# Starting the K-stack transfers from ScalarE, at steps 1 and 7 of a unit, in place of the SP queue

## The chip, the cores and the metric

The kernel runs on one core of a Trainium2 chip. The metric is the device time in microseconds (us) of one execution; lower is better.

## What is computed

One gated cross-attention layer and one gated feed-forward layer, over 8 batches of 224 tokens of width 1024, with a context of 8 x 750 tokens. Cut to what matters:

```python
q = x @ Wq.T;  k_raw = context @ Wk.T;  v_raw = context @ Wv.T      # 32 heads of 32
q = _rmsnorm(q);  k = _rmsnorm(k)                                   # per head
attn = softmax(einsum('bhnd,bhmd->bhnm', q, k) * HEAD_DIM ** -0.5)
out = einsum('bhnm,bhmd->bhnd', attn, v)
x = x + tanh(g_xattn[0]) * xattn(layernorm(x), ctx, Wq, Wk, Wv)
hidden = sigmoid(h @ Q(w1).T) * (h @ Q(w2).T)                        # h = layernorm(x), Q: ternary weights
x = x + tanh(g_ffn[0]) * (hidden @ Q(w3).T)
```

## The kernel before

There are three phases. Phase A projects the queries and stores them in DRAM. Phase B, which holds the change, projects keys and values and attends. The last phase is the feed-forward layer.

Phase B runs over 32 units, `u` = 0 to 31: four groups `g` of eight heads, each over eight batches `b`. A unit has 24 steps `r`, written as `t, j = r // 4, r % 4`: six context tiles `t` of 125 tokens, and four steps `j` for each. In every step TensorE does a quarter of the projection of tile `t` of unit `u` (L1255), then the scores of an earlier unit's piece (L1273), then the products of attention weights and values of a still earlier piece (L1297, L1300). The scores of unit `u - 1` begin at step 8 of unit `u` (`SHIFT`), and the value products trail them by three steps (`LAG`). Two more rounds, `k == U` and `k == U + 1`, finish the attention; in them nothing is projected.

All engines run their own program in order and are coupled by semaphores alone. In a step, piece `e` of the scores goes through this chain: scores on TensorE (step e + 8), `exp` on ScalarE (L831, same step), `phi`, its 16-bit high half, on ScalarE (L822, one step later), `plo`, the rest, on VectorE (L1102, same step as `phi`), and the value products on TensorE (step e + 11). At steps with `j == 1` ScalarE also rounds the next context tile (`chi`, L755) ahead of `phi`, and VectorE subtracts (`clo`, L987) ahead of `plo`. At steps with `j == 3` ScalarE copies `val` (L797) and `knat` (L801) ahead of `phi`; at steps 7 and 15 VectorE also sums a weight block (`gsum`, L1096) ahead of `plo`.

The normalised keys of a tile are transposed and copied by VectorE into `kpair` (L1083, at `j == 2` two tiles later). From there four DMAs in each of two parts gather them into `kst`, the K stacks that the scores read: part 0 holds tiles 0 to 3 of a unit (four DMAs of 250 KB), part 1 tiles 4 and 5 (four DMAs of 125 KB). Tile 3 of unit `u - 1` is in `kpair` after step 22 of unit `u - 1`; tile 5 after step 6 of unit `u`. TensorE waits for part 0 at step 8 and for part 1 at step 10 of unit `u` (L1266).

All DMAs go through the SP queue (`@block.sync`), in program order. For a unit `u` it issues: context loads `craw` for each `t` (L337, each waits until VectorE is done with the slot), at `t == 1` the save of an attention result (L354) and in the last five units a layer-norm save and load (L385, L386, L375, L379, called `ln_save` and `ln_load`), at `t == 2` a weight block `gbuf` (L430), at `t == 3` part 0 and at `t == 4` part 1 of the K stacks of unit `u - 1` (L396), then again `ln_save` and `ln_load`, and at `t == 5` eight loads of `qT` (L416), which wait until the scores of unit `u - 2` are over at step 7. The layer-norm tiles of batches that are finished are worked in units 27 to 31 (`ln` is true), in the gaps of the attention work.

Of the kernel before, what the change touches and what calls it, by code (L numbers as in the profile page):

```python
# [21 lines left out]
KT, KW = 6, 125  # L22
G, HG = 4, 8
GC = HG * DH
U = G * B
NQ = 4 * KT
# [5 lines left out]
HD2 = 2 * DH  # L32
# [24 lines left out]
def flamingo_kernel(nc, x_d, ctx_d, wq_d, wkv_d, wffn_d, gates_d, out_d):  # L57
# [8 lines left out]
    def sem(name):  # L66
        return top.enter_context(nc.semaphore(name))

    def sb(scope, name, shape, dt):
        return scope.enter_context(nc.sbuf_tensor(name, shape, dt))  # L70

    with top:
# [57 lines left out]
        kst = sb(pb, "kst", [P, 2, HG, SK], F16)  # L130
# [15 lines left out]
        kpair = sb(pb, "kpair", [P, 2, NP, SK], F16)  # L146
# [58 lines left out]
        kst_in = [[sem(f"kst_in{i}_{h}") for h in range(2)] for i in range(2)]  # L205
# [7 lines left out]
        s_ready = sem("s_ready"); p_ready = sem("p_ready"); phi_ready = sem("phi_ready")  # L213
# [39 lines left out]
        def projects(k):  # L253
            return k < U
# [53 lines left out]
        def _(sp):  # L308
# [25 lines left out]
            def load_ctx(T, slot, idx):  # L334

                wait(sp, clo_ready, T - 2)
                sp.dma_start(craw[:, slot, :, :], ctx_d[idx, :, :, :]).then_inc(ctx_in[slot], 16)  # L337
# [11 lines left out]
            def save_att(a, par, qts=(0, 1)):  # L349
                sp.wait_ge(att_ready, 2 * a + 1 + qts[-1])  # L350
                for qt in qts:
                    r0, r1 = QSAVED[qt]
                    q0 = QCOLS[qt].start
                    sp.dma_start(att_d[a, q0 + r0:q0 + r1, :],  # L354
                                 oatt[r0:r1, par, qt, :, :].rearrange("p h d -> p (h d)")
                                 ).then_inc(att_saved[par], 16)

            def load_w(j, s):

                for m in range(3):  # L360
                    sp.dma_start(wraw[:, 1 - s, m, :], wffn_d[m * (FJ // 2) + j, :, s, :]).then_inc(w_in[s], 16)

            def ln_load(i):

                s, b = ln_slot(i), i // 2
                if ln_slot(i) == 0:
                    sp.wait_ge(wklo_ready, KC * G)
                else:
                    sp.wait_ge(kv_ready, KT * U)


                sp.wait_ge(att_saved[b % 2], 32 * (((G - 1) * B + b) // 2 + 1) - (16 if i == NL - 2 else 0))
                wait(sp, ln_saved[s], 32 * ln_uses(i))
                cx, ca, _ = ln_mem[s]
                sp.dma_start(cx[:, :], x_d.rearrange("i p d -> (i p) d")[i * LT:i * LT + LT, :]  # L375
                             ).then_inc(lx_in[s], 16)
                for g in range(G):
                    r0 = LT * (i % 2)
                    sp.dma_start(ca[:, GC * g:GC * g + GC], att_d[g * B + b, r0:r0 + LT, :]).then_inc(lx_in[s], 16)  # L379

            def ln_save(i):
                s = ln_slot(i)
                _, ca, cn = ln_mem[s]
                sp.wait_ge(cnl_ready, i + 1)
                sp.dma_start(x1_d[i * LT:i * LT + LT, :], ca[:, :]).then_inc(ln_saved[s], 16)  # L385
                sp.dma_start(cn_d[i * LT:i * LT + LT, :, :], cn[:, :, :]).then_inc(ln_saved[s], 16)  # L386

            def stack_k(v, part):

                t0, t1 = ((0, 4), (4, KT))[part]  # L390
                sp.wait_ge(kpair_ready, v * KT + t1)
                if v >= 2:
                    sp.wait_ge(s_ready, (v - 1) * NQ)
                for i in range(2):
                    for s in range(2):
                        sp.dma_start(kst[HD2 * i:HD2 * i + HD2, v % 2, s:HG:2, KW * t0:KW * t1],  # L396
                                     kpair[HD2 * s:HD2 * s + HD2, v % 2, :, KW * t0:KW * t1]
                                     ).then_inc(kst_in[v % 2][part], 16)

            def unit_b(u, par, k, b, g, ln):  # L400
                if projects(k):
                    for t in range(KT):
                        if k or t >= 3:
                            load_ctx(u * KT + t, (par * KT + t) % 3, b * KT + t)
                        if t == 3 and k >= 1:
                            stack_k(u - 1, 0)
                        if t == 4 and k >= 1:
                            stack_k(u - 1, 1)
                        if t == KT - 1:
                            if k >= 2:  # L410

                                sp.wait_ge(s_ready, (u - 1) * NQ)
                            for i in range(4):
                                for s in range(2):
                                    r0 = HD2 * s + DH * (i // 2)
                                    sp.dma_start(qT[DH * i:DH * i + DH, par, s:HG:2, :],  # L416
                                                 qst_d[g, :, r0:r0 + DH, b * S:b * S + S].rearrange("p r t -> r p t")
                                                 ).then_inc(q_in[par], 16)
                        if t == 1 and k >= 2 and not (isinstance(u, int) and u == 2):
                            save_att(u - 3, 1 - par)  # L420
                        if ln and t in (1, 4):

                            i = 2 * (b - LNLAG) + t // 4
                            if i:
                                ln_save(i - 1)
                            ln_load(i)
                        if t == 2:
                            if k >= 2:
                                sp.wait_ge(gsum_ready, u * 2 - 2)
                            sp.dma_start(gbuf[:, par, :, :], wffn_d[u, :, :, :]).then_inc(gw_in[par], 16)  # L430
                if k == U:
                    load_ctx(U * KT, 0, 0)
                    stack_k(U - 1, 0)
                    sp.wait_ge(gsum_ready, 2 * U - 2)
                    sp.dma_start(gbuf[:, 0, :, :], wffn_d[U, :, :, :]).then_inc(gw_in[0], 16)
                if k == U:
                    save_att(U - 3, 1)
                    stack_k(U - 1, 1)
                    for i in (10, 11):
                        ln_load(i)  # L440
                    ln_save(9)
                    save_att(U - 2, 0)
                    for i in (12, 13):
                        ln_load(i)
                    sp.wait_ge(gsum_ready, 2 * WPAIRS)
                    for i in range(2):
                        for h in range(2):
                            sp.wait_ge(kst_in[i][h], 64 * (U // 2))
                    sp.wait_ge(v3_ready, KT * U + 1)
                    load_w(0, 0)  # L450
                    ln_save(10)
                    ln_save(11)
# [6 lines left out]
            for u in range(U):  # L459
                g = u // B  # L460
                unit_b(u, u % 2, min(u, 2), u % B, g, u >= (G - 1) * B + LNLAG)
                if u == 0 or (u % B == 1 and 0 < g < G - 1):
                    prefetch_w(g + 1)
            unit_b(U, 0, U, None, None, False)
            unit_b(U + 1, 1, U + 1, None, None, False)


# [87 lines left out]
        def _(pool):  # L555
# [96 lines left out]
            def ln_low(i):  # L652
                cx, _, cn = ln_mem[ln_slot(i)]
                pool.wait_ge(cnh_ready, i + 1)
                pool.tensor_tensor(cn[:, 1, :], cx[:, :], cn[:, 0, :], ALU.subtract).then_inc(cnl_ready, 1)  # L655
# [25 lines left out]
        def _(act):  # L681
# [15 lines left out]
            def w_high(g, kcs=range(KC)):  # L697

                act.wait_ge(wk_in, g * 16 + 16)
                if g:  # L700
                    act.wait_ge(kv_ready, g * (B * KT))
                for kc in kcs:
                    act.activation(wkhi[:, kc, :], wkraw[:, kc, :], ACT.Copy).then_inc(wkhi_ready, 1)
# [43 lines left out]
            def ln_high(i):  # L747
                cx, _, cn = ln_mem[ln_slot(i)]
                act.wait_ge(cn_ready, i + 1)
                act.activation(cn[:, 0, :], cx[:, :], ACT.Copy).then_inc(cnh_ready, 1)  # L750
# [8 lines left out]
            def group_b(g):  # L759
                if not (isinstance(g, int) and g == 0):  # L760
                    w_high(g)

            def unit_b(u, par, k, b, g, ln):
                for r in range(NQ):
                    t, j = r // 4, r % 4

                    Tb = u * KT + (t - 1)
                    pt = (par * KT + t - 1) % 2
# [66 lines left out]
                    if j == (1 if ln else 3):  # L835
                        for i in ln_tiles(u, k, t, ln, "norm"):
                            ln_high(i)

            units(act, unit_b, group_b)


# [578 lines left out]
```

## Time and profile before

| | us |
|---|---|
| median of three runs (2708.07 to 2711.51) | 2710.05 |
| the profiled execution, its own time | 2711.99 |
| its span in the trace | 2710.2 |
| TensorE busy | 2588.1 |
| VectorE busy | 1658.9 |
| ScalarE busy | 1454.9 |
| mean granted TensorE clock, share of full | 0.977 |

The span begins at the first and ends at the last instruction of the trace; the execution's own time is 1.79 us longer. Phase B lasts from about 230 to about 1845 us. Busy time does not hold instructions that issue DMAs.

### The profile page before, as it was taken

The numbers are of one execution on the slowest core, as the hardware profiler recorded it, in microseconds if no ns is written. First come the engines' busy times: TensorE is split into PE (matmuls) and PEld (weight loads), VectorE is DVE, ScalarE is ACT, GpSimd is POOL, SyncE is SP. The second block draws the span as 40 slices with busy tenths as digits, with TensorE's granted clock in tenths as the row PEclk, the third lists the DMA queues.
The fourth block names the chain that finished last, engine by engine and source line by source line (L and its number), as shares of the span: only waits on it lengthen the run. The fifth ranks groups of instructions, "written<-read, shape, count | busy, mean of one in ns | idle before, by whom it ended". The sixth has DMA issues, their size and how long they took to land.

```text
span 2710.2 us, 49526 instructions
## 1 busy us (share of the span) xinstructions
PE 2588.1 (95%) x18370; PEld 1872.0 (69%) x18370; DVE 1658.9 (61%) x2808; ACT 1454.9 (54%) x3102; POOL 928.8 (34%) x865
## 2 busy tenths in 40 slices
PE   7998999999999999999999988875899999999999
PEld 6776888888888888888888877663455455554444
DVE  5665777777777787777777877775544444430000
ACT  3333888888788888878788766673211111110000
POOL 3552344545445444454544755665000000000000
PEclk9998999999999999999999999986999999999999
DMA  4226455555544546446454566757423333334441
GB/s 154 79 63 199 113 152 130 135 127 150 152 125 137 134 114 182 125 131 136 120 151 125 147 163 182 183 140 235 161 96 100 109 107 107 93 98 137 148 123 71
DMA packets 274321, 361.45 MB, mean 133 GB/s; under 512 B 113569, under 2 KB 222625, under 8 KB 269345
## 3 DMA queue, kind: packets, MB, share of 16 engines
q1 hardware_dynamic: 274080, 358.29, 47.0%
q8 instruction: 146, 2.39, 0.4%
q14 instruction: 95, 0.77, 0.1%
HBM read 252.17 MB, written 56.89 MB: 114 GB/s over the span
## 4 chain that ended last, share of the span: by engine, by line
issue 35%; POOL 31%; PE 30%; DMA 2%; DVE 1%; SPq 0%; POOLq 0%; ACT 0%; DVEq 0%
PE ps L1350 19%; POOL krs L607 13%; PE ps L1377 10%; POOL oinv L628 4%; POOL osum L623 3%; POOL kms L603 3%; POOL qrs L585 2%; POOL osum L626 2%; POOL oatt L633 1%; DMA stage<-x_normalised 1%; POOL oinv L630 1%; POOL qms L582 1%; DMA attention<-oatt 1%; POOL cn L655 0%; DMA wraw<-in_wffn 0%
## 5 line engine op out<-in xcount | busy, mean ns | idle before, releaser
L1255 PE MATMUL ps<-wkhi,chi 128*125 128x512 f32 x1536 | 671.3, 437 | 8.9 <-DVE wklo L910 5.0
L1255 PE MATMUL ps<-wkhi,clo 128*125 128x512 f32 x1536 | 610.3, 397 | 0.0
L1255 PE MATMUL ps<-wklo,chi 128*125 128x512 f32 x1536 | 609.6, 397 | 0.0
L1102 DVE TENSOR_TENSOR plo<-pf,phi 125x448 f16<-125x448 f32 x768 | 545.6, 711 | 88.4 <-ACT phi L822 86.9
L831 ACT ACTIVATE pf<-ps 125x448 f32<-125x448 f32 x768 | 418.9, 545 | 291.2 <-PE ps L1273 288.1
L1350 PE MATMUL ps<-xnTh,w12q 128*128 128x512 f16 (+1 forms) x1408 | 481.6, 356 | 3.8 <-ACT xnTh L847 3.8
L1350 PE MATMUL ps<-xnTl,w12q 128*128 128x512 f16 (+1 forms) x1408 | 480.8, 355 | 0.0
L822 ACT ACTIVATE phi<-pf 125x448 f16<-125x448 f32 x768 | 443.9, 578 | 5.3
L1297 PE MATMUL ps<-val,phi 125*128 125x97 bf16 x3072 | 337.1, 210 | 37.7 <-DVE plo L1102 37.5
L607 POOL TENSOR_TENSOR krs<-kms,mhalf 125x8 f32<-125x8 f32 x192 | 345.7, 1801 | 15.1 <-POOL kms L603 0.2
L1255 PEld LDWEIGHTS ps<-wkhi,clo 128*125 128x125 f32 x1536 | 287.1, 187 | 73.7
L987 DVE TENSOR_TENSOR clo<-craw,chi 128x1000 fp32r<-128x1000 f32 x193 | 231.6, 1200 | 170.5 <-ACT chi L755 170.5
L1300 PE MATMUL ps<-val,plo 125*128 125x65 bf16 x3072 | 323.9, 195 | 0.0
L603 POOL TENSOR_TENSOR kms<-kss,rmseps 125x8 f32<-125x8 f32 x192 | 72.3, 377 | 732.0 <-DVE kss L1057 732.0
L1255 PEld LDWEIGHTS ps<-wkhi,chi 128*125 128x125 f32 x1536 | 288.1, 188 | 48.4 <-issue 9.8
L1255 PEld LDWEIGHTS ps<-wklo,chi 128*125 128x125 f32 x1536 | 289.7, 189 | 38.3
L1297 PEld LDWEIGHTS ps<-val,phi 125*128 125x128 f16 x3072 | 265.8, 98 | 44.9 <-DVE plo L1102 38.8
L1273 PE MATMUL ps<-qT,kst 128*125 128x224 f16 x1536 | 277.8, 263 | 17.6 <-DMA kst<-kpair 17.6
L1273 PEld LDWEIGHTS ps<-qT,kst 128*125 128x125 f16 x1536 | 207.1, 137 | 125.3 <-DMA kst<-kpair 20.0
L1377 PE MATMUL ps<-w3q,hid 128*128 128x512 bf16 x1232 | 266.1, 379 | 1.0 <-DVE hf L1136 1.0
L1300 PEld LDWEIGHTS ps<-val,plo 125*128 125x128 f16 x3072 | 252.0, 99 | 0.5
L861 ACT ACTIVATE sg<-ps 128x512 f32<-128x512 f32 x88 | 47.9, 544 | 357.3 <-PE ps L1350 357.3
(95 smaller groups left out, 3302.6 us busy)
## 6 DMA issues: line engine op xcount, KB each, us to landing
craw<-in_ctx SPq DMA_DIRECT2D x193, 500.0 KB, 4.5
gbuf<-in_wffn SPq DMA_DIRECT2D x33, 1024.0 KB, 6.9
wraw<-in_wffn SPq DMA_DIRECT2D x66, 512.0 KB, 5.8
kst<-kpair SPq DMA_DIRECT2D x128, 250.0 KB, 7.3
hid<-hidden SPq DMA_DIRECT2D x7, 2816.0 KB, 12.5
hidden<-hh SPq DMA_DIRECT2D x66, 256.0 KB, 2.1
kst<-kpair SPq DMA_DIRECT2D x128, 125.0 KB, 2.5
qT<-q_pairs SPq DMA_DIRECT2D x256, 56.0 KB, 3.2
```

The lines of the kernel that those rows point to most:

```text
L603: pool.tensor_tensor(kms[0:KW, :], kss[0:KW, :], rmseps[0:KW, 0:HG], ALU.add).then_inc(kms_ready, 1)
L607: pool.tensor_tensor(krs[0:KW, :], kms[0:KW, :], mhalf[0:KW, 0:HG], ALU.pow).then_inc(krs_ready, 1)
L822: act.activation(phi[0:KW, e % 6, :, :], pf[0:KW, e % 6, :].rearrange("p (t n) -> p t n", t=2), ACT.Copy).then_inc(phi_ready, 1)
L831: act.activation(pf[0:KW, e % 6, :], bank(3 + e % 3)[0:KW, 0:2 * S], ACT.Exp, bias=LN128, scale=SCALE).then_inc(p_ready, 1)
L987: dve.tensor_tensor(clo[:, par, :, :], craw[:, slot, :, :], chi[:, par, :, :].bitcast(F32), ALU.subtract).then_inc(clo_ready, 1)
L1102: dve.tensor_tensor(plo[0:KW, e % 6, :, :], pf[0:KW, e % 6, :].rearrange("p (t n) -> p t n", t=2), phi[0:KW, e % 6, :, :], ALU.subtract).t ...
L1255: mm = pe.matmul(bank(pt)[0:KW, :], a[:, pt, kc, :], w[:, kc, :], start=(kc == 0 and n == 0), stop=(kc == KC - 1 and n == 2))
L1273: mm = pe.matmul(bank(3 + e % 3)[0:KW, S * n:S * n + S], kst[:, ap, hd, KW * kt:KW * kt + KW], qT[:, ap, hd, :], start=True, stop=True)
L1297: mm = pe.matmul(o[:, c0:c0 + VW], phi[0:KW, sl, n, q], val[0:KW, vp, kt, hd, :], start=(e % 6 == 0 and qt == 0 and n == 0), stop=False, s ...
L1300: mm = pe.matmul(o[:, c0 + DH:c0 + VW], plo[0:KW, sl, n, q], val[0:KW, vp, kt, hd, DH:VW], start=False, stop=(e % 6 == 5 and n == 1), skip ...
L1350: mm = pe.matmul(o, w12q[:, s, m, kc, :], xt[:, kc, c0:c0 + n], start=(kc == 0 and part == 0), stop=(kc == KC - 1 and part == 1))
L1377: mm = pe.matmul(bank(4 * par + 2 * tt + c), hid[par][:, j, part, P * tt:P * tt + P], w3q[:, j, 512 * c:512 * c + 512], start=(j == 0 and ...
```

## The change

`stack_k` moves from the SP program to the ScalarE program. The two waits and the four DMAs of a part are the same; the engine that issues them is another, and so is the place in its order: part 0 of unit `u - 1` is begun at step 1 of unit `u`, ahead of everything that ScalarE does in that step, and part 1 at step 7.

```diff
-            def stack_k(v, part):
-                t0, t1 = ((0, 4), (4, KT))[part]
-                sp.wait_ge(kpair_ready, v * KT + t1)
-                if v >= 2:
-                    sp.wait_ge(s_ready, (v - 1) * NQ)
-                for i in range(2):
-                    for s in range(2):
-                        sp.dma_start(kst[...], kpair[...]).then_inc(kst_in[v % 2][part], 16)
...
-                        if t == 3 and k >= 1:
-                            stack_k(u - 1, 0)
-                        if t == 4 and k >= 1:
-                            stack_k(u - 1, 1)
...
-                    stack_k(U - 1, 0)
...
-                    stack_k(U - 1, 1)
...
+            def stack_k(v, part):          # in the ScalarE program
+                t0, t1 = ((0, 4), (4, KT))[part]
+                act.wait_ge(kpair_ready, v * KT + t1)
+                if v >= 2:
+                    act.wait_ge(s_ready, (v - 1) * NQ)
+                for i in range(2):
+                    for s in range(2):
+                        act.dma_start(kst[...], kpair[...]).then_inc(kst_in[v % 2][part], 16)
...
             def unit_b(u, par, k, b, g, ln):
                 for r in range(NQ):
                     t, j = r // 4, r % 4
+                    if r in (1, 7) and 1 <= k <= U:
+                        stack_k(u - 1, r // 7)
```

## Rows read from the trace of the kernel before

**Rows 1.** The page's first part: busy time, share of the span, instructions.

```profile
PE 2588.1 (95%) x18370; PEld 1872.0 (69%) x18370; DVE 1658.9 (61%) x2808; ACT 1454.9 (54%) x3102; POOL 928.8 (34%) x865
```

**Rows 2.** Waits, whole run: in total, times, longest (us).

```profile
PE ps L1273 <- DMA kst<-kpair: 17.6, 5, 6.7
```

**Rows 3.** Waits of PE from 1526 to 1800 us, same columns.

```profile
PE ps L1273 <- DMA kst<-kpair: 16.2, 4, 6.7
PE ps L1297 <- DVE plo L1102: 12.6, 11, 2.3
```

**Rows 4.** Busy time by window: length, then each engine, PEclk, DMA share, GB/s.

```profile
1526.16:1580.00 53.84, 50.65 (x424) 41.91 (x423) 43.61 (x77) 40.78 (x90) 35.16 (x30) 0.99 0.58 166
1580.00:1638.50 58.50, 53.38 (x409) 43.35 (x410) 44.38 (x77) 39.99 (x89) 34.54 (x30) 0.92 0.65 173
1638.50:1699.11 60.61, 50.93 (x409) 41.62 (x409) 45.77 (x77) 40.50 (x90) 35.18 (x30) 0.94 0.64 169
1699.11:1756.41 57.30, 51.84 (x409) 42.14 (x409) 43.73 (x77) 40.27 (x89) 34.91 (x30) 0.95 0.67 173
1040.84:1089.07 48.23, 48.23 (x413) 40.28 (x409) 37.14 (x69) 38.70 (x87) 22.72 (x22) 1.00 0.59 176
```

**Rows 5.** Timeline, steps 0 to 3 of one unit: start, duration, instruction, idle before.

```profile
1028.54 0.55 ACT L831 ACTIVATE pf<-ps 125x448 f32<-125x448 f32 x1 [0.40 <-PE ps L1273]
1028.98 1.03 ACT L755 ACTIVATE chi<-craw 128x1000 fp32r<-128x1000 f32 x1
...
1030.04 1.20 DVE L987 TENSOR_TENSOR clo<-craw,chi 128x1000 fp32r<-128x1000 f32 x1 [0.91 <-ACT chi L755]
...
1031.16 0.62 DVE L1102 TENSOR_TENSOR plo<-pf,phi 125x448 f16<-125x448 f32 x1
...
1032.66 0.54 ACT L831 ACTIVATE pf<-ps 125x448 f32<-125x448 f32 x1 [1.01 <-PE ps L1273]
...
1034.32 0.10 PEld L1297 LDWEIGHTS ps<-val,phi 125*128 125x128 f16 x1
```

**Rows 6.** Timeline of the SP queue, DMA issues of three stretches.

```profile
1024.43 3.96 SPq L396 DMA_DIRECT2D kst<-kpair  x4
...
1044.13 3.76 SPq L416 DMA_DIRECT2D qT<-q_pairs  x8
...
1795.31 3.24 SPq L396 DMA_DIRECT2D kst<-kpair  x4
```

**Rows 7.** Timeline, steps 6 to 10 of the same unit.

```profile
1040.40 0.41 DVE L1083 COPY kpair<-ps 128x500 f16<-128x500 f16 x1
1040.69 0.55 ACT L831 ACTIVATE pf<-ps 125x448 f32<-125x448 f32 x1 [0.56 <-PE ps L1273]
...
1040.84 2.59 SPq L396 DMA_DIRECT2D kst<-kpair  x4
1041.13 0.42 ACT L797 ACTIVATE val<-vres 125x256 bf16<-125x256 f32 x1
...
1043.06 0.62 DVE L1102 TENSOR_TENSOR plo<-pf,phi 125x448 f16<-125x448 f32 x1
...
1046.30 0.10 PEld L1297 LDWEIGHTS ps<-val,phi 125*128 125x128 f16 x1
...
1048.12 0.36 PEld L1273 LDWEIGHTS ps<-qT,kst 128*125 128x125 f16 x2
```

**Rows 8.** Timeline of a late unit: SP queue, ScalarE and TensorE.

```profile
1629.70 3.90 SPq L396 DMA_DIRECT2D kst<-kpair  x4
...
1634.68 1.04 ACT L755 ACTIVATE chi<-craw 128x1000 fp32r<-128x1000 f32 x1 [2.69 <-DMA craw<-in_ctx]
...
1646.56 0.63 PE L1273 MATMUL ps<-qT,kst 128*125 128x224 f16 x2 [6.68 <-DMA kst<-kpair]
```

**Rows 9.** DMA issues, 1629.6 to 1647 us: count, KB each, us to landing.

```profile
kst<-kpair SPq DMA_DIRECT2D x4, 250.0 KB, 10.3
```

**Rows 10.** Busy time in part of the round `k == U`, columns as in Rows 4.

```profile
1796.20:1811.12 14.92, 9.48 (x129) 7.02 (x126) 11.99 (x23) 13.04 (x30) 2.58 (x3) 0.88 0.82 215
```

More of the change, by code:

```diff
@@ L386, in ln_save @@
                 sp.dma_start(cn_d[i * LT:i * LT + LT, :, :], cn[:, :, :]).then_inc(ln_saved[s], 16)
-            def stack_k(v, part):
-                t0, t1 = ((0, 4), (4, KT))[part]
-                sp.wait_ge(kpair_ready, v * KT + t1)
-                if v >= 2:
-                    sp.wait_ge(s_ready, (v - 1) * NQ)
-                for i in range(2):
-                    for s in range(2):
-                        sp.dma_start(kst[HD2 * i:HD2 * i + HD2, v % 2, s:HG:2, KW * t0:KW * t1],
-                                     kpair[HD2 * s:HD2 * s + HD2, v % 2, :, KW * t0:KW * t1]
-                                     ).then_inc(kst_in[v % 2][part], 16)
             def unit_b(u, par, k, b, g, ln):
@@ L761, in group_b @@
                     w_high(g)
+            def stack_k(v, part):
[5 more added lines that the diff above has]
+                    for s in range(2):
+                        act.dma_start(kst[HD2 * i:HD2 * i + HD2, v % 2, s:HG:2, KW * t0:KW * t1],
+                                     kpair[HD2 * s:HD2 * s + HD2, v % 2, :, KW * t0:KW * t1]
+                                     ).then_inc(kst_in[v % 2][part], 16)
             def unit_b(u, par, k, b, g, ln):
```

## The prediction

> **What bounds the kernel now.** I read the page first: TensorE is busy for 2588.1 of 2710.2 us [rows 1]. The windows sharpen that. In a unit in the middle of phase B (1040.84 to 1089.07) it is busy for all of the 48.23 us, at full clock, while ScalarE has 38.70 us and VectorE 37.14 us of work [rows 4]. So in 26 of the units, 1 to 26, nothing that arrives earlier can help, and what arrives later costs only if it makes TensorE wait. Then I read the waits. TensorE waits for the K stacks 5 times in the whole run, 17.6 us together [rows 2], and 4 of these, 16.2 us, lie between 1526 and 1800 us [rows 3], where the layer-norm tiles share the queue. The four windows there are 53.84, 58.50, 60.61 and 57.30 us long [rows 4]. Against 4 x 48.23 = 192.9 us they take 230.3, an excess of 37.3 us. TensorE is idle in them for 3.2 + 5.1 + 9.7 + 5.5 = 23.5 us; the other 13.8 us go with a granted clock of 0.92 to 0.99 of full, that is with stretches at 1.2 in place of 2.4 GHz, which lie behind the waits. That is the only place with something to win. The last thing to read is the slack of the chain in the full units, from the timeline, since ScalarE is given new work there.
>
> **What the change removes.** SP is rid of 8 issues in a unit. It is not the bound in a full unit, so this is worth nothing there. What it removes in the late units is the queue ahead of part 0: in the unit shown SP began its four issues at 1629.70, behind a layer-norm save and load, two context loads and a weight block [rows 8], and they took 10.3 us to land [rows 9], in a stretch in which TensorE then stood for 6.68 us at the score matmul of step 8 [rows 8]. ScalarE reaches step 1 of that unit near 1628, by the steps of 2 us back from 1638.5, and needs no SP for it. The start is only some 1.5 us earlier, but the transfers have a queue of their own and need not let the layer-norm load, the two context loads and the weight block, 2.9 MB by the sizes of their tiles, pass first.
>
> The DMA page of the Trainium skill, "DMA: Bandwidth & Descriptors", section "Issuing engines are not separate DMA queues", says that DMAs of all issuing engines run on the same 16 DMA engines and interleave. By that rule alone the K stacks would take bandwidth from what SP loads beside them, and the bytes of the burst would be over no sooner.
>
> So for the late units I do not take the 16.2 us whole. The gain is 16.2 us if part 0 is always there at step 8. Against it: the context tile for step 5 already comes 2.69 us late [rows 8], and with 1 MB of K beside it it comes later; I take 1.5 us of it as visible in each of four units, 6 us, between nothing and the 2.69 us once again (10.8). I leave 1 us of K wait. ScalarE's own delay, below, comes to 5 x 0.6 = 3 us in units 27 to 31. Of the 13.8 us of lowered clock a part returns in proportion to the idle time: idle falls from 23.5 to about 23.5 - 16.2 + 6 + 1 + 3 = 17.3 us, so about 3.6 us. Sum: -16.2 + 6 + 1 + 3 - 3.6 = **-10 us**. Bounds: -16.2 - 9.5 = -26 (all waits for K gone and 16.2/23.5 of the clock loss with them), and +3 (the wait is only renamed, and ScalarE's delay comes on top).
>
> **What the change adds to a full unit.** No row shows ScalarE issuing a DMA, so its price comes from the same instructions on SP. Part 1 takes 2.59 us for four [rows 7]. Part 0 takes 3.96 us in a full unit [rows 6], where a weight block and a context load are under way in the same queue, and 3.24 us at 1795.31 [rows 6], where the issue before it lies 14 us back. ScalarE's queue will be empty as it is there, so I take 3.24 for part 0, between 2.6 and 4.1 us, and 2.6 for part 1. That is 5.84 us in a unit of 48.23 in which ScalarE has 9.5 us free [rows 4]: on the mean it fits. Does it fit where it lies?
>
> Step 1. In the unit shown `exp` of step 0 starts at 1028.54, and `chi` of step 1 at 1028.98, `clo` at 1030.04, `plo` at 1031.16 for 0.62 us, so until 1031.78; the value products that need it begin with the weight load at 1034.32 [rows 5]. The slack is 2.54 us. In the new order the four issues stand between `exp` and `chi`. If they may begin as soon as `exp` has started, `chi` starts at 1028.54 + 3.24 + some 0.05 = 1031.83, 2.85 us late, and TensorE stands for 2.85 - 2.54 = 0.3 us. If they begin only when `exp` has ended (1029.09), `chi` starts at 1032.33, 3.35 us late, and the stand is 0.8 us. I take the middle, 0.55 us. With 2.6 us for the four it is nothing to 0.2; with 4.1 us it is 1.2 to 1.7. Behind `chi` wait `phi`, `exp` and, on VectorE, `clo` and `plo` of this step. All of these are late by the same time. ScalarE has 1.01 us of idle at step 2 [rows 5] and some tenths in each step after it, and 9.5 - 5.84 us in the unit remain, so it has caught up before step 7.
>
> Step 7. `kpair` is ready at 1040.81 and `exp` of step 6 starts at 1040.69 [rows 7], so the wait itself costs at most 0.1 us. The issues end at 1040.81 + 2.62 = 1043.43, or 1041.24 + 2.62 = 1043.86 if they wait for `exp`. `val`, now at 1041.13 [rows 7], comes 2.3 to 2.7 us late, and through `gsum` so does `plo`, which ends at 1043.68 and is needed at 1046.30: a slack of 2.62 us [rows 7]. TensorE stands for 0 to 0.1 us; I take 0.05. The part itself must land before the scores of step 10, at 1048.12 [rows 7]. Its last issue ends some 2.6 to 3 us later than ScalarE reaches step 7, that is by 1043.9, with 4.2 us left to land: enough.
>
> Together 0.6 us in a unit, over 26 units: **+16 us**. Bounds: 0 (both fit) and 26 x 1.8 = +47.
>
> **The round k == U.** Nothing is projected there, and ScalarE is busy for 13.04 of 14.92 us [rows 10]: it is the bound, and has 1.9 us free. The 5.84 us of issues lie on its path, less about 1 us of that free time: **+5 us**, between 3 and 7. The one K wait there, 17.6 - 16.2 = 1.4 us, I leave in.
>
> **The sum.** +16 - 10 + 5 = +11 us. Against the profiled execution's own 2711.99 us that is 2723 us; this execution is 1.9 us above the median of the runs, so for the median I say **2721 us**, slower by 0.4%. A measurement of this kernel tells about 0.2%, 5.4 us, from no change.
>
> **The rivals.** *It is faster.* ScalarE's issues take 2.6 us in either part and start behind the start of `exp`, so `chi` is 2.3 us late against 2.54 of slack: no stand in any full unit. It decides from a price below some 0.63 us for one issue. Then the late units give their 10 us and the 3 us of delay there as well, up to 20 in all, and the round `k == U` costs 4: 2710 - 13 = 2697 us (2694 to 2704). For it: slack and price are equal within a few tenths. Against it: part 0 took 3.24 us for four where nothing was ahead of it [rows 6]. 0.18.
>
> *It makes no measurable difference.* Stands of 0.2 to 0.4 us in a full unit (5 to 10 us in all) and 5 us at the end are paid by the late units: 2705 to 2715 us. 0.17.
>
> *The issues are dearer on ScalarE than in any quiet row.* Part 0 costs 4.1 us as beside other loads, and at step 7 ScalarE's four issues meet SP's eight loads of `qT`, which are freed at the end of the same step and take 3.76 us for eight [rows 6], or 0.47 each. If two of ScalarE's wait for one of these each, part 1 is 0.9 us later and the stand there about 0.9 us. With 1.4 at step 1 that is 2.3 us in each of 26 units, 60 us, and 7 in the round `k == U`, less 5 in the late units: 2772 us; with one of the two, 2735 to 2750. The Trainium skill has a rule that would do just this: "Perfetto Trace Analysis", section "DMA Instruction — HWDGE (DVE, Sync)", has a descriptor generator that is shared between two issuing sequencers and locked for one of them at a time. No row here shows two issuers at once. 0.13.
>
> *The forecast*, a small stand in each full unit that outweighs the late units: 0.52.
>
> **How the numbers follow.** Faster than 2704.6: 0.18 and a little of the wash, 0.20. Within 0.2%: 0.16. Slower: 0.64. The likeliest case alone runs from 2716 to 2735 us. For 8 in 10 I take 2698 to 2752: it leaves out the lower end of the fast rival and the upper half of the dear one.
>
> **What the profile of the changed kernel would show.** ScalarE's queue has 256 DMA issues, near 0.65 us for one of part 1 and 0.8 for one of part 0. In a full unit `chi` of step 1 starts some 3 us behind `exp` of step 0, VectorE waits for `chi` for 3 to 4 us there, and TensorE has a wait for `plo` of 0.3 to 0.8 us at step 3, and next to none at step 9; the unit is 48.8 us long. The waits for the K stacks between 1526 and 1800 us are 1 us or less, those of ScalarE for `craw` longer than 2.7 us, and the four windows there sum to 220 us in place of 230. The prediction is wrong if full units stay at 48.23 us (issues cheaper or slack larger), if they exceed 49.5 us (issues dearer), or if the late units are no shorter (the K stacks were late for want of bandwidth, and not of a place in the queue).

## The result, and the profile after

The changed kernel takes 2733.72 us in the median of four runs (2729.65 to 2734.46), against 2709.06 before. The ratio is 1.0087, with a 95% interval of 1.0069 to 1.0104: slower by 24 us, where I forecast 11 in a range of -12 to +42. The profiled execution has a span of 2731.9 us.

First the waits of TensorE in the stretch in which units 28 to 31 now lie, to be held against [rows 3]: total, times, longest.

```profile
PE ps L1293 <- DVE plo L1098: 27.5, 17, 3.5
```

The waits for the K stacks, 16.2 us, are gone. Waits for `plo` have taken their place: 27.5 us against 12.6. Inside the four units alone, from step 6 of unit 27 to step 6 of unit 31, it is 12.5 us of K waits and 10.2 of `plo` before, and 27.4 of `plo` after; the fourth K wait, 3.7 us, lies behind step 6 of unit 31. Next the same four units by window, from step 6 to step 6, columns as in [rows 4].

```profile
1544.17:1602.98 58.81, 52.34 (x423) 42.62 (x422) 43.15 (x77) 39.42 (x88) 34.89 (x30) 0.97 0.58 172
1602.98:1662.49 59.51, 51.11 (x409) 41.51 (x409) 42.68 (x77) 39.31 (x88) 35.14 (x30) 0.97 0.58 170
1662.49:1720.68 58.19, 52.58 (x409) 42.57 (x410) 43.16 (x77) 39.43 (x88) 34.91 (x30) 0.94 0.59 173
1720.68:1780.84 60.16, 52.24 (x409) 42.37 (x410) 43.11 (x77) 39.41 (x88) 34.86 (x30) 0.95 0.60 168
```

They sum to 236.7 us against 230.3: longer by 6.4, where I had a gain of 10. TensorE is idle in them for 28.4 us against 23.5. To see where the rest is, take the copies of the last tile of a unit into `kpair`, from the timeline of VectorE. They are those of units 0, 25, 30 and 31 after,

```profile
264.72 0.41 DVE L1079 COPY kpair<-ps 128x500 f16<-128x500 f16 x1
...
1493.48 0.41 DVE L1079 COPY kpair<-ps 128x500 f16<-128x500 f16 x1
...
1780.43 0.41 DVE L1079 COPY kpair<-ps 128x500 f16<-128x500 f16 x1
...
1831.17 0.41 DVE L1079 COPY kpair<-ps 128x500 f16<-128x500 f16 x1
```

and the same four before.

```profile
264.75 0.41 DVE L1083 COPY kpair<-ps 128x500 f16<-128x500 f16 x1
...
1476.99 0.41 DVE L1083 COPY kpair<-ps 128x500 f16<-128x500 f16 x1
...
1755.97 0.41 DVE L1083 COPY kpair<-ps 128x500 f16<-128x500 f16 x1
...
1805.28 0.41 DVE L1083 COPY kpair<-ps 128x500 f16<-128x500 f16 x1
```

| stretch | before | after | difference | forecast |
|---|---|---|---|---|
| 25 full units (step 6 of unit 1 to step 6 of unit 26) | 1212.2 | 1228.8 | +16.5 | +16 (26 units) |
| the five units after them | 279.0 | 287.0 | +8.0 | -10 |
| to step 6 of the round `k == U` | 49.3 | 50.7 | +1.4 | +5 for this row |
| from there to the end of the span | 904.9 | 900.7 | -4.2 | and the next |

The chain in a full unit looks as the forecast drew it. This is the timeline of steps 0 to 3 of a unit after, all engines, to be held against [rows 5].

```profile
1135.33 0.54 ACT L827 ACTIVATE pf<-ps 125x448 f32<-125x448 f32 x1 [0.40 <-PE ps L1269]
1135.39 3.42 ACTq L753 DMA_DIRECT2D kst<-kpair  x4
1138.91 1.04 ACT L737 ACTIVATE chi<-craw 128x1000 fp32r<-128x1000 f32 x1 [3.04 <-issue]
...
1139.98 1.20 DVE L983 TENSOR_TENSOR clo<-craw,chi 128x1000 fp32r<-128x1000 f32 x1 [4.06 <-ACT chi L737]
...
1141.10 0.62 DVE L1098 TENSOR_TENSOR plo<-pf,phi 125x448 f16<-125x448 f32 x1
...
1141.77 0.10 PEld L1293 LDWEIGHTS ps<-val,phi 125*128 125x128 f16 x1 [0.63 <-DVE plo L1098]
```

The four issues begin 0.06 us behind the start of `exp`, while it still runs, and take 3.42 us; `chi` comes 3.58 us behind `exp` in place of 0.44, so 3.14 us late. Against the 2.54 us of slack [rows 5] that is 0.60 us too much, and the weight load stands for 0.63. The same sight at step 7, in the same unit:

```profile
1148.13 0.54 ACT L827 ACTIVATE pf<-ps 125x448 f32<-125x448 f32 x1 [0.55 <-PE ps L1269]
1148.29 2.71 ACTq L753 DMA_DIRECT2D kst<-kpair  x4
1151.05 0.43 ACT L793 ACTIVATE val<-vres 125x256 bf16<-125x256 f32 x1 [2.37 <-PE ps L1269]
```

`val` starts 2.92 us behind `exp` in place of 0.44 [rows 7]: 2.48 us late, inside the 2.62 of slack.

In a late unit the picture is another. This is the timeline of POOL, VectorE and ScalarE after, in the unit that answers to [rows 8].

```profile
1655.90 2.39 POOL L624 TENSOR_TENSOR ca<-ca,cx 112x1024 f32<-112x1024 f32 x1 [9.92 <-DMA ca<-attention]
...
1658.32 1.29 DVE L970 BATCH_NORM_STATS2 cst<-ca 112x6 f32<-112x512 f32 x2 [4.76 <-POOL ca L624]
...
1662.08 0.41 DVE L1079 COPY kpair<-ps 128x500 f16<-128x500 f16 x1
...
1662.52 2.62 ACTq L753 DMA_DIRECT2D kst<-kpair  x4
1665.18 0.42 ACT L793 ACTIVATE val<-vres 125x256 bf16<-125x256 f32 x1 [4.78 <-issue]
```

Read it from the top. The layer-norm input, which SP loads at `t == 1`, lands late, so POOL adds late; VectorE stands 4.76 us at the statistics of step 4, which its order puts ahead of `clo`, `plo` and the `kpair` copy of step 6. ScalarE had begun its last `exp` at 1659.84, ended it at 1660.40, and now waits for that copy until 1662.52, then issues for 2.62 us. Only then come `val`, `knat` and `phi`. SP's half is in its own timeline: before,

```profile
1621.45 0.43 SPq L386 DMA_DIRECT2D x_normalised<-cn  x1
1625.98 0.32 SPq L375 DMA_DIRECT2D cx<-in_x  x1
1626.34 1.84 SPq L379 DMA_DIRECT2D ca<-attention  x4
...
1628.22 0.43 SPq L337 DMA_DIRECT2D craw<-in_ctx  x1
```

and after, with part 0 of the K stacks begun by ScalarE at 1642.91:

```profile
1642.05 0.43 SPq L386 DMA_DIRECT2D x_normalised<-cn  x1
1646.80 0.32 SPq L375 DMA_DIRECT2D cx<-in_x  x1
1647.16 3.50 SPq L379 DMA_DIRECT2D ca<-attention  x4
1650.70 0.43 SPq L337 DMA_DIRECT2D craw<-in_ctx  x1
```

The four issues of `ca` take 3.50 us in place of 1.84, the context load that follows is 1.7 us later behind the first of them, and POOL's add starts 8.7 us after the first `ca` issue in place of 5.0 (1631.38 before). It is so in all four units, and only for the load beside part 0: at `t == 1` of units 28 to 31 the add comes 7.4, 8.7, 8.2 and 9.5 us after the first `ca` issue, against 5.5, 5.0, 6.4 and 4.9 before; at `t == 4`, with no K stack begun near it, 5.7, 5.3, 6.1 and 5.6 against 6.5, 4.9, 5.9 and 5.5. ScalarE's waits in this stretch, after (for `craw` it was 19.4 us in the four units before):

```profile
ACT chi L737 <- DMA craw<-in_ctx: 31.4, 8, 4.6
ACT val L793 <- issue: 21.7, 5, 5.6
```

### The profile page after: what moved, and what is told of

Same layout as the page of the kernel before. It is cut to its first block, busy times and chain, and to the rows that moved or that the text cites. A ratio compares the mean times of both kernels' runs of the same rounds, so it can differ in the third digit from the quotient of the medians.

```text
span 2731.9 us, 49526 instructions
## 1 busy us (share of the span) xinstructions
PE 2597.0 (95%) x18370; PEld 1874.1 (69%) x18370; DVE 1641.5 (60%) x2808; ACT 1432.7 (52%) x3102; POOL 919.7 (34%) x865
## 4 chain that ended last, share of the span: by engine, by line
issue 35%; PE 30%; POOL 29%; DMA 2%; DVE 2%; ACT 1%; POOLq 0%; SPq 0%; ACTq 0%; DVEq 0%
PE ps L1346 19%; POOL krs L589 13%; PE ps L1373 10%; POOL oinv L610 4%; POOL kms L585 3%; POOL osum L605 3%; POOL qrs L567 2%; POOL osum L608 2%; POOL oatt L615 1%; DMA stage<-x_normalised 1%; POOL oinv L612 1%; POOL qms L564 1%; DVE plo L1098 1%; DMA attention<-oatt 0%; PE ps L1251 0%
## 5 line engine op out<-in xcount | busy, mean ns | idle before, releaser
L1098 DVE TENSOR_TENSOR plo<-pf,phi 125x448 f16<-125x448 f32 x768 | 538.5, 702 | 61.9 <-ACT phi L818 61.7
L1269 PE MATMUL ps<-qT,kst 128*125 128x224 f16 x1536 | 279.0, 264 | 1.6 <-DMA kst<-kpair 1.6
L737 ACT ACTIVATE chi<-craw 128x1000 fp32r<-128x1000 f32 x193 | 200.8, 1041 | 124.7 <-issue 81.5
## 6 DMA issues: line engine op xcount, KB each, us to landing
hid<-hidden SPq DMA_DIRECT2D x7, 2816.0 KB, 12.5
```

What stands on the lines that cost most here:

```text
L737: act.activation(chi[:, par, :, :], craw[:, slot, :, :], ACT.Copy).then_inc(chi_ready, 1)
L1098: dve.tensor_tensor(plo[0:KW, e % 6, :, :], pf[0:KW, e % 6, :].rearrange("p (t n) -> p t n", t=2), phi[0:KW, e % 6, :, :], ALU.subtract).t ...
L1269: mm = pe.matmul(bank(3 + e % 3)[0:KW, S * n:S * n + S], kst[:, ap, hd, KW * kt:KW * kt + KW], qT[:, ap, hd, :], start=True, stop=True)
```

## The experiments

Two theories for what the forecast missed in the late units. *Crowding*: part 0, on its own queue at step 1, slows the layer-norm load and the context tiles that are under way beside it. *ScalarE's stand*: what is lost is ScalarE's time at step 7, waiting for `kpair` and issuing. For full units the theory is the slack of the forecast; its rival is that ScalarE's added work counts wherever it lies. "Late four" is the time from step 6 of unit 27 to step 6 of unit 31 in the one profiled execution; where nothing was changed there (before, full units only, last round only) it was 230.2, 229.7 and 227.4 us, so differences under 3 us say nothing. Each kernel is told by its difference from the kernel before. "Measured" is the ratio to that kernel, run beside it, with a 95% interval. The length of a full unit is the median of 25; before, it is 48.25 us, in the changed kernel 48.90.

**Part 0 alone on ScalarE.**

```diff
-  if t == 3 and k >= 1:                        # SP
+  if t == 3 and k >= 1 and not on_act(u, 0):   # SP; the same for part 1 and for k == U
+  if r == (1, 7)[part] and 1 <= k <= U and on_act(u, part):   # ScalarE
+      stack_k(u - 1, part)
+def on_act(u, part): return part == 0
```

> Only part 0 (step 1) is begun by ScalarE, part 1 stays on the SP queue. If the cost of a full unit is the slack of 2.54 us at step 1 and nothing at step 7, full units stay at 48.85 us as in the changed kernel, +16 us in all. If both steps cost, 48.5 us. Late units: the theory that part 0, begun at step 1 on its own queue, crowds out the layer-norm load and the context tile says that units 28 to 31 stay near 236 us for four, as in the changed kernel; the theory that ScalarE's standing at step 7 (up to 5 us there) is the loss says they fall below 225. Total 2732 by the first, 2718 by the second.

Measured: 1.0035 (1.0025 to 1.0045). A full unit takes 48.84 us, the late four 224.4. So nearly all of what a typical full unit loses is lost at step 1. The sum over 25 units is 11.5 us above before, though, and not 16.5; the rest is told below. The late units came out as the theory of ScalarE's stand says: part 0 by itself costs nothing there.

**Part 1 alone on ScalarE** (`return part == 1`).

> Only part 1 (step 7) is begun by ScalarE. Full units: 48.25 us as before if step 7 has the slack that the rows of before give (2.62 us against 2.3 to 2.7). Late units: by crowding at step 1 they are as before, 230 us for four, K waits included, total 2709 to 2712. By the rival, ScalarE standing at step 7, they are 5 to 10 us longer than before, total 2715 to 2720.

Measured: 1.0013 (1.0004 to 1.0022). Full units 48.26 us (1.4 us over 25 of them), late four 230.8, with 13.0 us of K waits still there. Step 7 has the slack that the forecast gave it. In the late units this is what crowding says, not the stand: by itself part 1 lengthens them by less than profiles differ. So neither theory holds alone. The runs leave part 1 3.5 us (1.1 to 6.0), of which the profile places only those 1.4.

**Full units alone** (`return u < 27`).

> Units 1 to 26 as in the changed kernel, units 27 to 31 and the last round as before. If the cost adds up by place: +16 us, full units 48.85, the late ones as before with their K waits of some 16 us, total 2725. If the late loss comes from what the full units hand over, the late units would be longer than 230 us for four here too.

Measured: 1.0054 (1.0034 to 1.0074), 14.6 us. Full units 48.87, late four 229.7 us. The costs add up by place, as far as the intervals tell.

**Units 27 to 31 alone** (`return 27 <= u < U`).

> Only units 27 to 31 as in the changed kernel. If the cost adds up by place: full units 48.25, the late four 236 us, total 2715 to 2718. My forecast of a gain of 10 us there would give 2700.

Measured: 1.0021 (1.0012 to 1.0030), 5.7 us slower. Late four 235.7 us. The waits of TensorE in them, from a window of their length:

```profile
PE ps L1318 <- DVE plo L1123: 29.2, 16, 4.3
```

**Part 0 early, on SP.** Nothing on ScalarE; in units 27 to 31 SP begins part 0 ahead of the layer-norm save.

```diff
   if t == 1 and k >= 2 and not (isinstance(u, int) and u == 2):
       save_att(u - 3, 1 - par)
+  if ln and t == 1:
+      stack_k(u - 1, 0)
...
-  if t == 3 and k >= 1:
+  if t == 3 and k >= 1 and not ln:
```

> Nothing on ScalarE. In units 27 to 31 the SP queue begins part 0 ahead of the layer-norm save and load of t == 1, so some 4 us before step 0 and not at step 3 or 4. ScalarE has no new work. If the late loss of the changed kernel is ScalarE's time, this one has the gain without the loss: K waits gone, four late units near 215 us, total 2695. If it is crowding (1 MB of K beside the layer-norm save and load), the layer-norm load is late here as well: K waits gone, waits for plo in their place, four late units 225 to 236 us, total 2704 to 2715.

Measured: 0.9991 (0.9981 to 1.0000). Late four 228.2 us, and this is what TensorE waited for in them:

```profile
PE ps L1320 <- DVE plo L1125: 22.5, 8, 5.1
```

No K wait is left and ScalarE has nothing new to do, yet `plo` takes the place of the K stacks. That part of the loss is not ScalarE's time.

**The same, with a quarter of part 0.** It leaves out three quarters of the rows of part 0 in units 27 to 31, so the scores there are not those of the layer.

```diff
+  n = 16 if part == 0 and U > v + 1 >= 27 else HD2
-  sp.dma_start(kst[HD2 * i:HD2 * i + HD2, ...], kpair[HD2 * s:HD2 * s + HD2, ...])
+  sp.dma_start(kst[HD2 * i:HD2 * i + n, ...], kpair[HD2 * s:HD2 * s + n, ...])
```

> As the kernel with part 0 early on the SP queue, but in units 27 to 31 the four transfers of part 0 move only 16 of their 64 partitions, a quarter of the bytes and of the packets; the scores of those units are computed from stale keys for the rest. The waits, the order and the number of transfers are the same. If the K traffic itself delays the layer-norm load and the context tiles (crowding), the waits for plo (24.0 us late in the kernel before this one) fall by more than half and the four late units from 228 to below 218 us. If the layer-norm chain is late by itself and the K waits only hid it, they stay at 226 to 229.

Measured: 0.9947 (0.9927 to 0.9967). Its windows and waits of TensorE in the late four, the window of the kernel with the whole of part 0 first:

```profile
1527.69:1755.84 228.15, 205.57 (x1636) 169.07 (x1634) 173.84 (x305) 160.90 (x353) 139.59 (x120) 0.94 0.60 177
```

```profile
1523.92:1741.27 217.35, 200.84 (x1645) 165.38 (x1645) 175.64 (x306) 161.03 (x353) 139.79 (x120) 0.98 0.58 172
```

```profile
PE ps L1321 <- DVE plo L1126: 15.5, 8, 3.0
```

Three quarters of the traffic of part 0 are worth 10.8 us in four units, with the same waits and the same number of issues: 6 us of idle time (22.6 to 16.5) and the rest while TensorE is busy, at a granted clock of 0.98 in place of 0.94. A part of it can be SP's time: its four issues take 2.6 us in place of 3.2 to 3.4. So crowding is real. But it is not the layer-norm load that is slow in this order: in unit 29 POOL's add comes 4.9 us after the first `ca` issue with the whole of part 0, and 5.3 with a quarter. The load begins late, since it waits until the layer-norm save that is under way beside part 0 has landed: it follows the second save by 5.7 us (1624.36 to 1630.05) against 4.6 (1616.07 to 1620.68). And the waits for `plo` fell by a third, not by more than half as crowding alone would have it: TensorE still waits 15.5 us for `plo` beside little traffic. That the layer-norm chain alone makes these is not shown.

**Part 0 alone, in units 27 to 31 alone.**

> Only part 0 and only in units 27 to 31 is begun by ScalarE. The kernel with part 0 alone had four late units of 224.4 us in one profile, 5.8 less than before. If that is real it returns here: 224 to 226, total 2704. If part 0 at step 1 is no better in late units than on SP, 229 to 231, total 2710.

Measured: 0.9979 (0.9969 to 0.9989), 5.7 us faster than before. Late four 226.7 us. With part 1 added, in the kernel above, it was 5.7 us slower: part 1 on ScalarE costs 11.4 us by the medians once part 0 is there too.

**Part 1 at step 8, in units 27 to 31** (`(1, 8)[part]`).

> Units 27 to 31 on ScalarE, part 0 at step 1 and part 1 at step 8. With part 1 at step 7 the four late units took 235.7 us, and ScalarE waited up to 2.7 us for kpair and then issued for 2.6. If the wait for kpair is the larger part of the 11 us that part 1 adds to part 0, they fall below 230 here; if the issuing is, they stay at 233 or more. K waits at step 10 may take the place.

Measured: 0.9995 (0.9986 to 1.0005), 7 us faster than with step 7; late four 232.5 us in the profile, 3 less. The profiled execution is the slowest of its ten, 5.9 us above their median, so the profile understates the gain. The place at step 7 is a good part of what part 1 costs, by the runs the larger one. How much of that is the wait for `kpair` and how much the issues ahead of `val`, `knat` and `phi` of step 7 isn't separated: the move to step 8 takes both away.

**The last round alone** (`return u == U`).

> Only the last round (k == U) on ScalarE. My forecast was +5 us for it, since ScalarE is the bound there. In the changed kernel the stretch from step 6 of unit 31 to the end of the trace took 952.6 - 1.1 us against 954.2 before, no longer. If that is real, the total is 2704 to 2708 here, because SP, rid of its wait for kpair at step 6, begins the layer-norm loads of tiles 10 and 11 at once; if ScalarE's time counts, 2712.

Measured: 0.9999 (0.9989 to 1.0009). No change that the runs can tell, and 5 us is ruled out.

**Part 0 at step 2** (`(2, 7)[part]`, part 1 on SP).

> Part 0 on ScalarE at step 2, behind chi of step 1, part 1 on SP. By the slack theory plo of step 2 ends 3.3 us ahead of its use and the four issues take 3.3 us: the stand of TensorE in a full unit falls from 0.6 to 0 to 0.15 us, full units 48.25 to 48.4, +0 to +4 us there. By the rival that ScalarE's share of work is what counts (5.9 or 3.3 us in a unit, wherever), full units stay at 48.6 or more. Late units as in the kernel with part 0 alone on ScalarE.

Measured: 1.0010 (1.0001 to 1.0019). A full unit takes 48.41 us, 0.16 over before in place of 0.59 at step 1, and 25 of them 1.5 us more in place of 11.5, although the four issues are dearer here (4.07 us in the median, 3.34 at step 1). The slack decides, not ScalarE's share of work. The late four took 230.7 us here, not 224.4; why step 2 is worse than step 1 there wasn't looked into.

**The context load ahead of the layer-norm save**, with late part 0 on ScalarE, and without anything on ScalarE.

```diff
-  if ln and t in (1, 4):
+  if ln and t in (2, 4):
```

> Part 0 on ScalarE in units 27 to 31 only, and there the SP queue issues the context load of t == 2 ahead of the layer-norm save and load of t == 1. In the kernel with late part 0 alone ScalarE waited 27.6 us for context tiles between 1525 and 1800 us. If it is the bytes under way that make them late, the earlier place brings that below 10 us and the four late units from 226.7 to 218 to 222, total 2697. If the layer-norm load is what holds VectorE at step 4, it stays at 225 to 228, since that load comes no sooner.

> Nothing on ScalarE; in units 27 to 31 the SP queue issues the context load of t == 2 ahead of the layer-norm save and load. The K stacks keep their place at the end of the queue, so their waits of some 16 us stay: four late units 226 to 230 us, total 2704 to 2708. If instead the K waits were only a cover of the late context tiles, they shrink together: 220 us.

Measured: 0.9980 (0.9970 to 0.9989) with part 0 on ScalarE, late four 225.7; 0.9966 (0.9953 to 0.9979) without, late four 222.4. With part 0 on ScalarE the second reading fits, in which the layer-norm load is what holds VectorE. Without it the time fell further than I gave it, since the K waits shrank with the late context tiles; in the late four TensorE waited for this:

```profile
PE ps L1318 <- DVE plo L1123: 11.3, 8, 2.2
PE ps L1294 <- DMA kst<-kpair: 9.5, 3, 3.7
```

ScalarE waited 9.8 us for context tiles between 1525 and 1800 us (21.2 before). With part 0 on ScalarE it waited 11.1 (27.6 in the kernel with late part 0 alone), and yet `plo` cost TensorE 22.9 us in its late four, against 23.4 there. So the late context tiles are not what makes TensorE wait once part 0 is on ScalarE. With the K stacks begun at step 1, an order of SP that is better by itself by 9 us gains nothing more. The kernel without anything on ScalarE has the lowest median of those that do the whole work, 2697.3 us.

## Why the prediction was right, and where it failed

The measured time lies inside the range, but only one of the three terms came out as forecast: +16 where I had +16, +6 in the late units where I had -10, and none that the runs can tell where I had +5.

*Full units: right, in mechanism and in size.* The forecast was a stand of 0.55 at step 1 and 0.05 at step 7; the units got 0.65 us longer, 16.5 us over 25 of them, in a typical unit nearly all from step 1 (part 0 alone 48.84 us, part 1 alone 48.26). Of the two readings of when the issues begin, the early one holds: 0.06 us behind the start of `exp`. The price of part 0 was too low for it: 3.42 us in the unit shown, against 3.24. The two errors cancel, so it is in part luck that the size is so near. The fast rival's condition, worked out again with issues that begin behind the start of `exp`, is a price below 0.73 us for one issue, (2.54 + 0.44 - 0.05) / 4, and not 0.63; part 0 took 0.84 (3.36 for four in the median), so it was not met either way. The issues of part 1 took 2.71 against 2.6. The move to step 2 showed that it is the place that costs.

*The dear rival came in three units only.* Part 1 took 2.60 to 2.76 us for four in most full units against 2.59 on SP, though two or three of SP's loads of `qT` are issued within that time. In four of 26 units it took 3.0 to 4.1, and three of these units are 49.4 to 50.1 us long in place of 48.9: by their lengths some 2.8 of the 16.5 us, most of what part 0 alone (11.5) and part 1 alone (1.4) leave open. In each of them one of the four issues is slow, 1.2 to 2.1 us in place of 0.65. On SP, with no second issuer, the four took up to 3.4 us too, so a second issuer is not what makes an issue slow, or not it alone. The 0.9 us that I took for two issues that wait came in none of the others. The Trainium skill, "Perfetto Trace Analysis", section "DMA Instruction — HWDGE (DVE, Sync)", names the sequencers of VectorE and SyncE as the two that share the descriptor generator. Whether ScalarE and SyncE share one so, no run here shows.

*Late units: wrong, +6.4 in the four windows in place of -10.* By the forecast's own sign, late units that are no shorter, this part is wrong; but the reason given there does not hold as it stands, since the K stacks did come in time. The step that failed is the list of what stands against the 16.2 us: 6 us for the context tile, 1 us of K wait, 3 us for ScalarE. Three things in it. First, I let the K stacks crowd only the context tile. In the changed kernel they also crowd the layer-norm load (8.7 us to POOL's add in place of 5.0), on which POOL's add hangs, on which VectorE's statistics at step 4 hang, ahead of all that VectorE does next. Behind this is a wrong reading of when ScalarE reaches step 1. I counted steps of 2 us back from 1638.5 and came to 1628, a start only some 1.5 us earlier; ScalarE's timeline of before has it at 1623.4,

```profile
1623.40 0.55 ACT L831 ACTIVATE pf<-ps 125x448 f32<-125x448 f32 x1 [0.40 <-PE ps L1273]
1623.85 1.03 ACT L755 ACTIVATE chi<-craw 128x1000 fp32r<-128x1000 f32 x1
```

which is 6.3 us ahead of SP's start, and ahead of the layer-norm load at 1625.98. So part 0 does not start beside the burst that SP had put in front of it, but before it: 1642.91 against 1646.80 in the changed kernel. In the order of SP that begins part 0 early too, three quarters of its traffic were worth 10.8 us in four units. Second, I costed the new wait at step 7 from a full unit, at 0.1 us. The `kpair` copy stands behind those statistics in VectorE's order, so in a late unit it comes up to 2.7 us behind the start of `exp`, ScalarE idles up to 2.1 us and then issues for 2.6, ahead of `val`, `knat` and `phi`. Third, a slip of size: I set the whole 16.2 us against the four windows, and 12.5 of them lie there. Part 0 alone gains 5.7 us in these units (3.0 to 8.4), over half of the 10 that I forecast for both; part 1 turns that into a loss of 5.7. Why part 1 alone costs little there was not tested; the K waits of before are then still in place, and its stand may lie beside them.

*The last round: wrong, 0 in place of +5.* ScalarE is the bound there by its busy share, and its two stands are in the trace, but alone they change the time by some 0.1% at most. The stretch up to step 6 is 1.4 us longer and the one behind it 4.2 us shorter. The kernels that left this round as it was took 44.7 to 47.9 us and 902.5 to 904.3 for the two, the one with the last round alone 53.0 and 903.0, so a single profile tells little here and the runs decide. SP no longer waits for `kpair` there and begins the next layer-norm loads earlier: at 1818.2, 13.0 us ahead of the copy of step 6, in place of 1808.4, 3.1 us behind it. That these pay for it is argued from that, not shown.

*The sum.* By the runs the parts are 14.6, 5.7 and -0.3, together 20.0; the whole is 24.7 us slower by the medians, 23.6 by the ratio, with an interval from 18.7 to 28.2. They agree within it. The forecast of 11 is 13 us too low; the late units are 16 of that, by the four windows, and the last round gives 5 back. That it lies in the range is owed to the width of the range and to errors that offset each other, as much as to the full units.

## What to carry to other kernels

A DMA issue is work of the engine that makes it: here four took 2.6 to 3.4 us in most full units and up to 4.5 in late ones, and on an engine with 9.5 us free in a unit they still cost 0.6 us, since the slack at that place was 2.54. Look at the slack of the chain behind the new place, not at the share of idle time, and try the next place over: one step later the cost was 0.16 us. Read the time of the new place from the timeline, in the stage in question; counted back by steps it was 4.6 us off here. Before a transfer is started earlier, list what else is under way then and who waits for it; and look up who writes what a moved wait waits for, in the busiest stage and not in the quiet one.

## What the runs showed of the hardware

ScalarE's issues began while its last activation was still running, 0.06 us behind its start at step 1, and the next activation followed 0.04 to 0.11 us behind the last issue in the lines shown. The fourth issue of part 0 is slow although nothing was issued on ScalarE's queue for 33 us before (1.15 us in the median of 26 units, the first 0.60): the four took 3.42 us in the unit shown, the four of part 1, with half the bytes, 2.71. That a queue of its own gives a transfer no bandwidth of its own is what the DMA page of the Trainium skill says ("DMA: Bandwidth & Descriptors", section "Issuing engines are not separate DMA queues"), and the trace agrees: the layer-norm load beside it took 8.7 us in place of 5.0 from its first issue to POOL's add. Of these 3.7 us, 1.7 are SP's own issues, which took 3.50 us in place of 1.84; why they are slow there, no run separates.
